# Splitting the softmax-denominator finish of an attention kernel into two steps, two strips apart

## The chip, the cores and the metric

One Trainium2 chip. The program runs on all 8 cores, each with one of the 8 batch elements and no exchange between them. The time is device time in microseconds (us) of the slowest core.

## The reference

One pre-norm transformer layer on x of 8 x 2048 x 1024 in f32. The first half is causal attention with 16 heads of 64 numbers and learned relative-position tables for keys and for values. The second half is a mixture of 8 experts of which each token takes the best one.

```
rel = jnp.tril(idx[:, None] - idx[None, :])
rk = embk[rel]
rv = embv[rel]
att = jnp.einsum('bhtd,bhsd->bhts', q, k) * scale + jnp.einsum('bhtd,tsd->bhts', q, rk)
att = jnp.where(causal[None, None], att, -jnp.inf)
att = jax.nn.softmax(att, axis=-1)
y = jnp.einsum('bhts,bhsd->bhtd', att, v) + jnp.einsum('bhts,tsd->bhtd', att, rv)
...
x = x + _L0_attn_ref(_layernorm(x, axis=-1), ...)
x = x + _L0_ffn_ref(_layernorm(x, axis=-1), ...)
```

The tables have 1024 entries, so a distance over 1023 reads the last one.

## The kernel before

Every instruction is written out by hand with the semaphores that it waits for, through one helper (`EM`, line 61 of the profile is its call). Each engine runs its instructions in the order in which they are written, so the order of the code is the order of each queue.

**Stages.** Layer norm and transposing of x; then for each group of 4 heads the projections to q, k, v; the attention of each of the 16 heads; the output projection; a second layer norm; the router; the experts (from about 3130 us on).

**A head.** It has a first part, in which q times the key table is computed for 16 row blocks, and stored to HBM (`prev_sb` to `prevh`). From there it is read back shifted by one element for each row, so that the distance becomes the position (`rel_sb`, loads on ScalarE's queue). Then come 16 strips of 128 query rows each, i = 0 to 15. Strip i does for each of its i // 4 + 1 chunks of 512 keys: TensorE makes scores (`ps_s<-qkv_sb`), VectorE adds `rel_sb` to them, ScalarE takes the exponential into `att_sb`. SyncE stores the strip shifted to `bmath`. The traversal of a strip (`trav_closure`) is written two strips later: TensorE transposes `att_sb` to `ps_t`, VectorE copies that to `attT_sb`, TensorE multiplies it with `vaug_sb` into `ps_y`. `vaug_sb` has v and two columns of ones, which give the sum of the exponentials, the softmax's denominator, in rows 64 and 65.

**The finish.** After strips 3, 7, 11 and 15, SyncE issues eight transposing loads of the stored exponentials (`bt_sb<-bmath`). Four strips later, ahead of strips 7, 11, 15 and of strip 3 of the next head, the finish of these four strips runs (`fin_closure`, line 640, kept in `pending_fin` with the strip at which it is due, lines 485 and 691):

- TensorE: eight matmuls `ps_y<-bt_sb,e_sb`, each waiting for its own load.
- ScalarE: `fin_sb<-ps_y`, copies the denominator rows out.
- VectorE: the cast `finb_sb<-fin_sb`, and the reciprocal `fin_sb<-fin_sb` of one row of 512.
- TensorE: `ps_y<-finb_sb,ev_sb`, the correction for distances beyond the table. Its wait is for VectorE's last instruction, the reciprocal.
- TensorE: `ps_s<-fin_sb,ones_f`, which replicates the reciprocal row to 64 partitions, in f32, into one of the four banks `ps_s` that the scores use in turn (`pool_alloc`).
- ScalarE: `rep_sb<-ps_s`, the copy of it; VectorE: `yT<-ps_y,rep_sb`, the multiplication.

There are two accumulators `ps_y`, which the groups of four strips use in turn, and 64 finishes in all. The finish of strips 8 to 11, for example, is ahead of strip 15; the accumulator that it frees is next written at the end of strip 2 of the next head.

Of the kernel before, what the change touches and what calls it, by code (L numbers as in the profile page):

```python
# [67 lines left out]
def build(debug=False):  # L68
# [33 lines left out]
    EM = P.emit  # L102

    with ExitStack() as gctx:
# [17 lines left out]
        cst_sb = E(nc.sbuf_tensor("cst_sb", [128, 8], F32))  # L122

        s_const = SM("s_const")
        s_pe = SM("s_pe")
        s_act = SM("s_act")
        s_dve = SM("s_dve")
# [39 lines left out]
        EM("vector", "memset", cst_sb[:, 4:5], -32.0, incs=[(s_dve, 1)])  # L167
        EM("vector", "memset", negbig_bf[:], NEGBIG, incs=[(s_dve, 1)])
        CONST_D = s_const.n
# [42 lines left out]
        with ExitStack() as actx:  # L212
# [23 lines left out]
               incs=[(s_dve, 1)])  # L236
            MS_D2 = s_dve.n

            for p in range(2):
                for g16 in range(16):  # L240
# [4 lines left out]
                       waits=([(s_dve, MS_D)] if (p == 0 and g16 == 0) else []),  # L245
                       incs=[(s_pg, 16)])
            PG_D = s_pg.n

            for p in range(2):
                for i8 in range(8):  # L250
# [4 lines left out]
                       waits=([(s_dve, MS_D)] if (p == 0 and i8 == 0) else []),  # L255
                       incs=[(s_bz[p], 16)])
# [6 lines left out]
            def pool_alloc():  # L263
                k = pool_ctr[0] % 4
                pool_ctr[0] += 1
                return k
# [8 lines left out]
            pending_fin = []  # L275
# [4 lines left out]
            fin_pe_guard = [0]  # L280
            plast_dve = [0]
# [6 lines left out]
            for i in range(NT):  # L288
# [5 lines left out]
                   waits=[(s_dve, xt_free[sl])], incs=[(s_x[sl], 16)])  # L294
# [9 lines left out]
            if debug:  # L304
                EM("gpsimd", "dma_start", out=dbg["dbg_xnT"], in_=xnT[:],
                   waits=[(s_act, P1_ACT)], incs=[(s_dbg, 16)])
# [17 lines left out]
            for g in range(4):  # L324
                par = 0
                wbase = 0
                for jout in range(6):
                    j3, mh = jout // 2, jout % 2
                    for tc in range(4):
# [7 lines left out]
                           waits=[(s_wq[0], wq_ready[g]), (s_act, max(P1_ACT, bg[0])),  # L337
                                  (s_dve, bg[1])],
                           incs=[])
# [26 lines left out]
                for hl in range(4):  # L366
                    h = 4 * g + hl
# [109 lines left out]
                    for i in range(NT):  # L477
# [147 lines left out]
                        if i % 4 == 3:  # L625
# [14 lines left out]
                            def fin_closure(tc=tc, ypar=ypar, h=h, hpar=hpar,  # L640
                                            btvals=tuple(btvals)):
                                for rt in range(8):
# [11 lines left out]
                                   waits=[(s_pe, max(yrel_pe, fin_pe_guard[0]))],  # L654
# [4 lines left out]
                                   incs=[(s_dve, 1)])  # L659
                                EM("vector", "reciprocal", fin_sb[64:65, 512:1024],  # L660
                                   fin_sb[64:65, 0:512], incs=[(s_dve, 1)])
                                fdv = s_dve.n
# [3 lines left out]
                                   waits=[(s_dve, fdv), (s_const, CONST_D)],  # L666
                                   incs=[(s_pe, 1)])
                                rbk = pool_alloc()
# [4 lines left out]
                                   waits=[(s_act, rbg[0]), (s_dve, rbg[1])],  # L673
# [17 lines left out]
                            pending_fin.append((gstrip + 4, fin_closure))  # L691

# [407 lines left out]
```

How the kernel before makes its waits and increments, by code:

```python
        def fn(h, method=method, args=args, kw=kw, wl=wl, il=il):  # L58
            for sh, v in wl:
                h.wait_ge(sh, v)
            ins = getattr(h, method)(*args, **kw)
            for sh, k in il:
                ins.then_inc(sh, k)
# [949 lines left out]
            def _final(h, OUT0=OUT0, OUT1=OUT1, DBG_D=s_dbg.n):  # L1013
                h.wait_ge(s_out[0].h, OUT0)
                h.wait_ge(s_out[1].h, OUT1)
                if DBG_D:
                    h.wait_ge(s_dbg.h, DBG_D)
```

## Time and profile before

| what | us |
|---|---|
| median of three runs | 5174.56 |
| the three runs | 5296.69, 5125.42, 5174.56 |
| the profiled execution | 5125.42 |
| its span, slowest core (core 0) | 5123.6 |
| spans of the eight cores | 5070.2 to 5123.6 |
| TensorE busy with matmuls | 3523.7 (69%) |
| VectorE busy | 1323.9 (26%) |
| ScalarE busy | 1283.8 (25%) |

The span runs from a core's first to its last instruction. PE is TensorE, PEld its weight loads, DVE VectorE, ACT ScalarE, SP SyncE; a q behind a name is an engine's sequencer, which issues transfers. In rows of groups the number behind the count is busy time, then the mean of one in ns, then the idle time of the engine just before them and what ended it. In rows of a timeline come the start, the length, the engine, the operation and in brackets the idle time before. Matmuls are pipelined: one that lasts 0.60 us makes room for the next after 0.43 to 0.47 us here.

### The profile page before, as it was taken

What the parts mean: (1) busy time and instruction counts of PE and PEld (TensorE: products, weight loads), DVE (VectorE), ACT (ScalarE), POOL (GpSimd) and SP (SyncE); (2) the same over time, 40 slices, a digit from 0 to 9 for tenths busy, and PEclk for the clock granted to TensorE, in tenths of its full rate; (3) what the DMA queues carried; (4) which work ended last, traced back from release to release, by engine and by line L of the source; (5) the groups of instructions that cost most, each with busy time, mean ns of one, the idle gap of its engine ahead of it and who ended that gap; (6) DMA issues with size and microseconds to landing.
All of it is one profiled execution on the core that took longest, in us unless ns stands there. A gap on an engine that the chain in (4) does not pass through costs nothing.

```text
span 5123.6 us, 48552 instructions; the slowest of 8 cores (5070.2 to 5123.6 us)
## 1 busy us (share of the span) xinstructions
PE 3523.7 (69%) x16065; PEld 1590.9 (31%) x16065; DVE 1323.9 (26%) x2366; ACT 1283.8 (25%) x2210; POOL 213.5 (4%) x373
## 2 busy tenths in 40 slices
PE   0455557555575566565665611999999999999992
PEld 0222223222232222222222200444444444444440
DVE  0134343434433444424444211001101110110011
ACT  3423223222222232233223042221121122112210
POOL 1000000000001000000000001000000000000002
PEclk9855556555565555565555855999999999999995
DMA  5255433443435333433444323130303113030303
GB/s 127 63 107 124 102 112 81 127 109 105 112 94 127 105 112 108 114 83 110 120 107 122 130 67 63 20 66 1 66 1 66 33 34 66 1 66 1 66 1 127
DMA packets 455408, 415.87 MB, mean 81 GB/s; under 512 B 304464, under 2 KB 353632, under 8 KB 455160
## 3 DMA queue, kind: packets, MB, share of 16 engines
q1 hardware_dynamic: 372992, 258.06, 18.2%
q0 software_dynamic: 45312, 76.06, 9.0%
q10 hardware_dynamic: 36864, 78.66, 6.1%
q8 instruction: 138, 2.26, 0.2%
q14 instruction: 102, 0.84, 0.1%
HBM read 264.16 MB, written 157.29 MB: 82 GB/s over the span
## 4 chain that ended last, share of the span: by engine, by line
PE 52%; DMA 15%; DVE 10%; SPq 7%; ACT 7%; issue 7%; POOL 1%; ACTq 1%; DVEq 0%; POOLq 0%
PE ps_h L61 17%; PE ps_v L61 17%; PE ps_s L61 9%; SPq L61 7%; PE ps_y L61 6%; DMA prevh<-prev_sb 6%; DVE fin_sb L61 4%; DMA bt_sb<-bmath 3%; DMA bmath<-att_sb 2%; DVE ps_s L61 2%; PE ps_t L61 2%; DMA xt_sb<-x 1%; ACT prev_sb L61 1%; DVE attT_sb L61 1%; ACT xn_sb L61 1%
## 5 line engine op out<-in xcount | busy, mean ns | idle before, releaser
L61 PE MATMUL ps_v<-w_sb,h_sb 128*128 128x512 bf16 x4096 | 889.2, 379 | 34.0 <-ACT h_sb L61 34.0
L61 PE MATMUL ps_h<-xn2T,w_sb 128*128 128x512 bf16 x4096 | 891.3, 380 | 30.1 <-DMA w_sb<-w 30.0
L61 ACT ACTIVATE h_sb<-ps_h,b1c_sb 128x512 bf16<-128x512 f32 x512 | 351.7, 687 | 1459.6 <-PE ps_h L61 1459.6
L61 DVE SCALAR_TENSOR_TENSOR acc_sb<-ps_v,g_sb,acc_sb 128x512 bf16<-128x512 f32 x256 | 192.4, 751 | 1649.0 <-PE ps_v L61 1649.0
L61 PEld LDWEIGHTS ps_v<-w_sb,h_sb 128*128 128x128 bf16 x4096 | 398.4, 98 | 524.8 <-issue 48.9
L61 PEld LDWEIGHTS ps_h<-xn2T,w_sb 128*128 128x128 bf16 x4096 | 400.9, 98 | 515.4 <-issue 33.9
L61 PE MATMUL ps_y<-attT_sb,vaug_sb 128*66 128x128 bf16 x2176 | 328.7, 305 | 289.9 <-DVE attT_sb L61 283.2
L61 ACT ACTIVATE att_sb<-ps_s,cst_sb 128x512 bf16<-128x512 f32 x640 | 395.3, 685 | 461.5 <-DVE ps_s L61 340.7
L61 DVE TENSOR_TENSOR ps_s<-ps_s,rel_sb 128x512 f32<-128x512 f32 (+3 forms) x624 | 386.4, 670 | 335.7 <-PE ps_s L61 327.0
L61 PE MATMUL ps_s<-embkRT_sb,qkv_sb 64*128 64x512 bf16 x448 | 202.7, 572 | 211.8 <-DVE plast_sb L61 108.4
L61 PEld LDWEIGHTS ps_y<-attT_sb,vaug_sb 128*66 128x66 bf16 x2176 | 228.7, 164 | 381.1 <-issue 378.2
L61 PE MATMUL ps_t<-eye_sb,att_sb 128*128 128x128 bf16 x2176 | 314.5, 308 | 14.3 <-ACT att_sb L61 14.3
L61 PE MATMUL ps_s<-qkv_sb 64*128 64x512 bf16 x640 | 312.9, 622 | 0.0
L61 DVE COPY attT_sb<-ps_t 128x512 bf16<-128x512 bf16 (+3 forms) x640 | 227.4, 379 | 303.0 <-PE ps_t L61 296.3
L61 PE MATMUL ps_y<-bt_sb,e_sb 128*66 128x512 bf16 x512 | 235.6, 597 | 90.4 <-DMA bt_sb<-bmath 89.7
L61 PEld LDWEIGHTS ps_t<-eye_sb,att_sb 128*128 128x128 bf16 x2176 | 218.4, 141 | 218.5 <-issue 218.5
L61 ACT CAST prev_sb<-ps_s 128x512 bf16<-128x512 f32 x256 | 146.5, 583 | 417.8 <-DMA prevh<-prev_sb 303.1
L61 PE MATMUL ps_y<-finb_sb,ev_sb 2*64 2x512 bf16 x64 | 38.2, 597 | 294.4 <-DVE fin_sb L61 294.4
L61 DVE RECIPROCAL fin_sb<-fin_sb 1x512 f32<-1x512 f32 x64 | 213.5, 3336 | 0.0
L61 DVE CAST prev_sb<-ps_s 128x512 bf16<-128x512 f32 (+1 forms) x192 | 119.8, 625 | 314.4 <-DMA prevh<-prev_sb 312.8
L61 PE MATMUL ps_s<-xnT,wqkv_sb 128*128 128x512 bf16 x768 | 172.0, 388 | 1.2 <-ACT xnT L61 1.2
L61 POOL DMA_DIRECT2D w_sb<-w x192 | 101.5, 592 | 1521.7 <-PE ps_h L61 1345.2
(83 smaller groups left out, 1401.2 us busy)
## 6 DMA issues: line engine op xcount, KB each, us to landing
w_sb<-w POOLq DMA_DIRECT2D x64, 512.0 KB, 13.5
w_sb<-w POOLq DMA_DIRECT2D x128, 256.0 KB, 10.8
prevh<-prev_sb SPq DMA_DIRECT2D x80, 384.0 KB, 2.3
rel_sb<-prevh ACTq DMA_DIRECT2D x80, 384.0 KB, 3.6
bmath<-att_sb SPq DMA_DIRECT2D x80, 384.0 KB, 3.0
xt_sb<-x SPq DMA_DIRECT2D x32, 512.0 KB, 4.0
rel_sb<-prevh ACTq DMA_DIRECT2D x64, 256.0 KB, 3.6
xt_sb<-x_spill SPq DMA_DIRECT2D x32, 512.0 KB, 3.8
```

Source lines behind the costliest of these rows:

```text
L61: ins = getattr(h, method)(*args, **kw)
```

## The change

The finish is written as two closures. The first, due at four strips as before, ends with the correction matmul, and that matmul waits for the cast alone. The second, due at six strips, has the replication, its copy and the multiplication; the replication now waits for its reciprocal by name. So the second halves stand ahead of strips 9, 13, and of strips 1 and 5 of the next head. ScalarE's copy into `fin_sb` waits also for the reciprocal of the finish before. One more constant is set at the start, which nothing reads.

```diff
+        EM("vector", "memset", cst_sb[:, 5:6], 0.0, incs=[(s_dve, 1)])
...
+            fin_war_dve = [0]
+            fin_rec = [0]
...
                                 EM("scalar", "copy", fin_sb[64:66, 0:512],
                                    ps_y[ypar][64:66, :],
-                                   waits=[(s_pe, max(yrel_pe, fin_pe_guard[0]))],
+                                   waits=[(s_pe, max(yrel_pe, fin_pe_guard[0])),
+                                          (s_dve, fin_war_dve[0])],
                                    incs=[(s_act, 1)])
...
+                                fdv_cast = s_dve.n
                                 EM("vector", "reciprocal", fin_sb[64:65, 512:1024],
                                    fin_sb[64:65, 0:512], incs=[(s_dve, 1)])
-                                fdv = s_dve.n
+                                fin_war_dve[0] = s_dve.n
+                                fin_rec[0] = s_dve.n
                                 EM("tensor", "matmul", ps_y[ypar][0:64, :],
                                    ev_sb[64:66, :], finb_sb[64:66, 0:512],
                                    start=False, stop=True, skip_group_check=True,
-                                   waits=[(s_dve, fdv), (s_const, CONST_D)],
+                                   waits=[(s_dve, fdv_cast), (s_const, CONST_D)],
                                    incs=[(s_pe, 1)])
+
+                            def fin_closure_b(tc=tc, ypar=ypar, h=h,
+                                              fin_rec=fin_rec):
                                 rbk = pool_alloc()
                                 rbg = pool_state[rbk]
                                 EM("tensor", "matmul", pool_banks[rbk][0:64, :],
                                    ones_f[64:65, :], fin_sb[64:65, 512:1024],
                                    start=True, stop=True,
-                                   waits=[(s_act, rbg[0]), (s_dve, rbg[1])],
+                                   waits=[(s_act, rbg[0]), (s_dve, fin_rec[0]),
+                                          (s_dve, rbg[1])],
                                    incs=[(s_pe, 1)])
...
                             pending_fin.append((gstrip + 4, fin_closure))
+                            pending_fin.append((gstrip + 6, fin_closure_b))
```

What the queues hold at the two kinds of place. TensorE in the first head, before: strip 13 with the traversal of strip 11 (first five rows), then further on the finish ahead of strip 15 and the strip's four scores.

```order
L61 MATMUL ps_s<-qkv_sb 128x512 x4
L61 MATMUL ps_t<-eye_sb,att_sb 128x128 x8
L61 MATMUL ps_y<-attT_sb,vaug_sb 66x128 x4
L61 MATMUL ps_t<-eye_sb,att_sb 128x128 x4
L61 MATMUL ps_y<-attT_sb,vaug_sb 66x128 x8
...
L61 MATMUL ps_y<-bt_sb,e_sb 66x512 x8
L61 MATMUL ps_y<-finb_sb,ev_sb 64x512
L61 MATMUL ps_s<-fin_sb,ones_f 64x512
L61 MATMUL ps_s<-qkv_sb 128x512 x4
```

The same two places after.

```order
L61 MATMUL ps_s<-fin_sb,ones_f 64x512
L61 MATMUL ps_s<-qkv_sb 128x512 x4
L61 MATMUL ps_t<-eye_sb,att_sb 128x128 x8
L61 MATMUL ps_y<-attT_sb,vaug_sb 66x128 x4
L61 MATMUL ps_t<-eye_sb,att_sb 128x128 x4
L61 MATMUL ps_y<-attT_sb,vaug_sb 66x128 x8
...
L61 MATMUL ps_y<-bt_sb,e_sb 66x512 x8
L61 MATMUL ps_y<-finb_sb,ev_sb 64x512
L61 MATMUL ps_s<-qkv_sb 128x512 x4
```

The replication `ps_s<-fin_sb,ones_f` has moved from behind the correction to the front of a strip: the one ahead of strip 13 belongs to the finish that began ahead of strip 11.

VectorE in the second head, from its first additions over the finish ahead of strip 3 to strip 5, before.

```order
L61 TENSOR_TENSOR ps_s<-ps_s,rel_sb 128x512 x3
L61 COPY attT_sb<-ps_t 128x128
L61 CAST finb_sb<-fin_sb 2x512
L61 RECIPROCAL fin_sb<-fin_sb 1x512
L61 TENSOR_TENSOR yT<-ps_y,rep_sb 64x512
L61 TENSOR_TENSOR ps_s<-ps_s,rel_sb 128x512
L61 COPY attT_sb<-ps_t 128x256
L61 TENSOR_TENSOR ps_s<-ps_s,rel_sb 128x512 x2
L61 COPY attT_sb<-ps_t 128x384
L61 TENSOR_TENSOR ps_s<-ps_s,rel_sb 128x512 x2
```

The same stretch after.

```order
L61 TENSOR_TENSOR ps_s<-ps_s,rel_sb 128x512
L61 TENSOR_TENSOR yT<-ps_y,rep_sb 64x512
L61 TENSOR_TENSOR ps_s<-ps_s,rel_sb 128x512 x2
L61 COPY attT_sb<-ps_t 128x128
L61 CAST finb_sb<-fin_sb 2x512
L61 RECIPROCAL fin_sb<-fin_sb 1x512
L61 TENSOR_TENSOR ps_s<-ps_s,rel_sb 128x512
L61 COPY attT_sb<-ps_t 128x256
L61 TENSOR_TENSOR ps_s<-ps_s,rel_sb 128x512 x2
L61 COPY attT_sb<-ps_t 128x384
L61 TENSOR_TENSOR yT<-ps_y,rep_sb 64x512
L61 TENSOR_TENSOR ps_s<-ps_s,rel_sb 128x512 x2
```

The reciprocal stays where it was, ahead of the next strip's addition. The multiplications `yT<-ps_y,rep_sb` stand now between the additions of strips 0 and 1 (for the finish ahead of strip 15 of the head before) and ahead of those of strip 5.

## Rows read from the trace of the kernel before

**Rows 1.** The page's chain that ended last, shares by engine and line.
```profile
PE 52%; DMA 15%; DVE 10%; SPq 7%; ACT 7%; issue 7%; POOL 1%; ACTq 1%; DVEq 0%; POOLq 0%
PE ps_h L61 17%; PE ps_v L61 17%; PE ps_s L61 9%; SPq L61 7%; PE ps_y L61 6%; DMA prevh<-prev_sb 6%; DVE fin_sb L61 4%; DMA bt_sb<-bmath 3%; DMA bmath<-att_sb 2%; DVE ps_s L61 2%; PE ps_t L61 2%; DMA xt_sb<-x 1%; ACT prev_sb L61 1%; DVE attT_sb L61 1%; ACT xn_sb L61 1%
```

**Rows 2.** Groups by shape, whole span: busy us, mean ns, idle before.
```profile
L61 PE MATMUL ps_y<-bt_sb,e_sb 128*66 128x512 bf16 x512 | 235.6, 597 | 90.4 <-DMA bt_sb<-bmath 89.7
...
L61 DVE RECIPROCAL fin_sb<-fin_sb 1x512 f32<-1x512 f32 x64 | 213.5, 3336 | 0.0
...
L61 PE MATMUL ps_y<-finb_sb,ev_sb 2*64 2x512 bf16 x64 | 38.2, 597 | 294.4 <-DVE fin_sb L61 294.4
```

**Rows 3.** Chain at a head's end, 1180 to 1345 us: start, length, what.
```profile
1188.99 2.37 DMA bmath<-att_sb
1191.44 2.01 SPq L61
...
1202.93 1.61 DMA prevh<-prev_sb
```

**Rows 4.** Timeline of the finish ahead of strip 15, 1336 to 1346 us.
```profile
1337.05 0.42 DVE L61 CAST finb_sb<-fin_sb 2x512 bf16<-2x512 f32 x1 [4.71 <-ACT fin_sb L61]
1337.39 3.34 DVE L61 RECIPROCAL fin_sb<-fin_sb 1x512 f32<-1x512 f32 x1
...
1340.88 0.60 PE L61 MATMUL ps_y<-finb_sb,ev_sb 2*64 2x512 bf16 x1 [4.59 <-DVE fin_sb L61]
...
1341.27 1.91 PE L61 MATMUL ps_s<-fin_sb,ones_f 1*64 1x512 f32 x2
...
1343.12 1.88 PE L61 MATMUL ps_s<-qkv_sb 64*128 64x512 bf16 x4
1343.27 0.58 ACT L61 COPY rep_sb<-ps_s 64x512 f32<-64x512 f32 x1 [6.33 <-PE ps_s L61]
...
1343.95 0.68 DVE L61 TENSOR_TENSOR yT<-ps_y,rep_sb 64x512 bf16<-64x512 f32 x1 [3.23 <-ACT rep_sb L61]
...
1344.56 0.74 DVE L61 TENSOR_SCALAR ps_s<-ps_s,plast_sb 128x512 f32<-128x512 f32 x1
```

**Rows 5.** Timeline of strip 13, 1320 to 1326 us.
```profile
1320.59 1.88 PE L61 MATMUL ps_s<-qkv_sb 64*128 64x512 bf16 x4
...
1321.30 0.43 DVE L61 TENSOR_TENSOR ps_s<-ps_s,rel_sb 128x256 f32<-128x256 f32 x1 [1.29 <-PE ps_s L61]
...
1323.82 0.75 DVE L61 COPY attT_sb<-ps_t 128x512 bf16<-128x512 bf16 x2
...
1324.39 0.61 PE L61 MATMUL ps_y<-attT_sb,vaug_sb 128*66 128x128 bf16 x4 [0.95 <-DVE attT_sb L61]
```

**Rows 6.** Timeline of a head's strips 0 to 2, 1237 to 1242 us.
```profile
1237.64 1.46 PE L61 MATMUL ps_s<-qkv_sb 64*128 64x512 bf16 x3
...
1238.36 1.90 DVE L61 TENSOR_TENSOR ps_s<-ps_s,rel_sb 128x512 f32<-128x512 f32 x3 [8.27 <-PE ps_s L61]
...
1240.36 0.23 DVE L61 COPY attT_sb<-ps_t 128x128 bf16<-128x128 bf16 x1
```

**Rows 7.** PE's waits in 2434:2443 (before strip 7), 2303:2317 and 1291.5:1301.5 (strip 11): total, times, longest.
```profile
PE ps_y L61 <- DMA bt_sb<-bmath: 2.0, 3, 1.3
...
PE ps_y L61 <- DMA bt_sb<-bmath: 0.3, 2, 0.2
...
PE ps_y L61 <- DMA bt_sb<-bmath: 4.7, 2, 2.4
```

**Rows 8.** The tile bt_sb: issue time in ns and landing in us, min/median/max.
```profile
L61 SPq DMA_TRANSPOSE bt_sb<-bmath x512: 1127/1261/3492, 278.2 to 2841.7; - x171
...
DMA to landing us min/median/max: 2.4/3.6/9.4
```

**Rows 9.** Windows: PE, PEld, DVE, ACT, POOL busy, granted clock, DMA share, GB/s.
```profile
1280.00:1360.00 80.00, 53.52 (x260) 27.20 (x260) 36.52 (x68) 21.10 (x36) 0.00 (x0) 0.54 0.53 109
...
1440.00:1520.00 80.00, 58.81 (x277) 29.31 (x278) 35.51 (x64) 24.03 (x40) 0.00 (x0) 0.60 0.44 112
```

## The prediction

> **What bounds the kernel now.** Read first the chain of work that ended last [rows 1]: TensorE (PE) holds 52%, but a third of that is the expert layers behind 3120 us, which the change does not touch. What matters are two items: "DVE fin_sb" with 4%, and "SPq" with 7%. The groups by shape come next [rows 2]. The reciprocal is one partition of 512 numbers, 3.34 us each, 64 of them, 213.5 us; 4% of 5124 us is 205, so nearly every one of them lies on the chain. The row of the matmul that reads finb_sb shows the same from PE's side: it stood idle 294.4 us before these 64, 4.6 us each.
>
> The timeline of one finish, the one ahead of strip 15, shows the order of things [rows 4]. The reciprocal runs from 1337.39 to 1340.73. PE then does the correction matmul (1340.88) and the replication matmul in f32 (1341.27, 1.91 us), and only then the scores of the strip (1343.12). ScalarE (ACT) copies the replicated row out (1343.27), VectorE (DVE) multiplies (1343.95), and DVE's first addition of the strip starts at 1344.56. So all three engines work on one thing after another here.
>
> Last, how a strip's exponentials reach the next event [rows 3]: at the end of a head they are followed by the store of att_sb, eight transposing loads that SyncE issues one by one from 1191.44, and the stores of prev_sb queued behind these at 1202.93. Each four strips inside a head have such a DMA chain too, and PE waits for its last piece: 89.7 us in 83 waits [rows 2].
>
> **The finish, first half.** After the change the correction matmul waits for the cast, which is over when the reciprocal starts, and PE goes on to the scores at once. For PE alone that brings the scores from 1343.12 to about the cast's end at 1337.47, plus 0.15 until PE has the signal and 0.39 for the correction: 1338.01, 5.1 us earlier [rows 4]. But the reciprocal keeps its place in DVE's queue, ahead of the additions, and PE's matmuls over attT_sb wait for a DVE copy that stands behind these additions. So the strip moves by what DVE gains: its first addition can start when the reciprocal ends, at 1340.73, and not at 1344.56. That is 3.83 us: the correction matmul, the replication, its copy and the multiplication. The reciprocal itself is not hidden. I take 3.83, the shift of the engine that ends last. The upper bound is PE's 5.1 us. Zero is excluded, since the reciprocals lie on the chain: the chain's 4% can be 3.5%, 179 of the 213.5 us, or 84% of them, and 84% of 3.83 is 3.2, the lower bound. It applies to 63 finishes (the 64th has no strip behind it; there only the correction matmul, 0.4 us, goes): 63 x 3.83 + 0.4 = 241.7 us. The exponentials of strips 3, 7, 11 and 15 come right behind a finish, so the DMA chains that they start move with them.
>
> **The second half, two strips later.** PE gets the replication ahead of the strip's scores, and DVE gets the multiplication ahead of its additions, behind ACT's copy. In rows 4 it takes 1344.56 - 1341.27 = 3.29 us from the replication's start to the first addition. Without it, at strip 13, it takes 1321.30 - 1320.59 = 0.71 us from scores to first addition [rows 5]. The price is 2.58 us where the DVE queue ends last, and it does there: the copy to attT_sb follows the additions (1323.82) and PE waits for it until 1324.39. It stands at strips 5, 9, 13 and 1 of the next head.
> - Strip 13: nothing covers it, since the finish ahead of strip 15 found its loads landed (there PE ran into them without a wait, its correction matmul follows at 1340.88). 16 x 2.58 = 41.3 us.
> - Strip 5: ahead of strip 7 PE waits for bt_sb anyway, at least 2.0 us [rows 7] and 58 us in the 16 heads. What is over the wait adds up to 1 us.
> - Strip 9: ahead of strip 11 these waits are 0.3 to 4.7 us [rows 7], 29 us in 16. Finish by finish, what 2.58 has over them adds up to 15.5 us.
> - Strip 1: three scores, three additions from 1238.36, a copy at 1240.36 [rows 6]. With the replication behind the first score (from 1238.07) the second addition starts at 1238.07 + 3.29 = 1241.36, the third 0.6 later, the copy at 1242.6: 2.2 us late. 15 x 2.2 = 33 us.
> Sum 91 us, with bounds 0 (all of it covered) and 63 x 2.58 = 163.
>
> **The rest.** The extra memset of a constant is one of six of its kind at the start and waits for nobody. The added wait of ACT's copy for an earlier reciprocal, and the replication's wait for its own, are met two strips before; behind them would stand the exponentials and the scores. A bank of ps_s is taken at another strip, one in four, free before the fourth score asks. These edits cost nothing, or at most their issue, below 0.1 us for each finish, 6 us.
>
> **Sum.** 241.7 - 91 = 150 us less. The profiled execution took 5125.4 us (span 5123.6): 4975. The median of the three runs, 5174.6, lies 49 above it: 5025 for a median of like runs. I set down 4995, between them. With the bounds of both halves the fastest is 5125 - 63 x 5.1 = 4804, the slowest 5125 - (63 x 3.2 - 163 - 6) = 5092, or 5141 on the scale of the median.
>
> **A rule of the clock.** The granted clock in this stage is 0.54 in one stretch of 80 us and 0.60 in another [rows 9], so mostly 1.2 GHz with patches of 2.4. The finishes' idle time on PE becomes shorter. The Trainium skill ("TensorE: Matmul & The Clock Gate", the part on HAM oscillation) says that an engine that keeps waiting between bursts falls back to half clock and pays the way up again, and one kept busy stays at full clock. By that the change could gain more than my sum. The trace agrees in that the stage with the gaps is the slow one, but PE's wait for the attT_sb copy remains in each strip.
>
> **Rivals.**
> 1. The second half costs its full price everywhere, as the DMA chain shrinks with the strips and covers nothing: 163 - 9 (strip 1 is cheaper) = 154, leaving 88 us: 5037, within 2%. For it: the waits at strip 11 are small. Against: a chain started by a strip has a length of its own. 15%.
> 2. The reciprocal is hidden whole (DVE's additions are not what ends last): 63 x 5.1 - 91 = 230, 4895. Against it stands the copy behind the additions [rows 5]. 5%.
> 3. The clock: if the stage went from 0.54 to 0.60, matmuls would take 10% less. PE's items ps_s, ps_y and ps_t on the chain are 17%, 871 us [rows 1]: 87 more gained, 4888. It is what the rule above would do here. 8%.
> 4. Slower: strips that come earlier push their bias loads into the eight transposing loads. Landing goes from 3.6 to the 9.4 us seen at worst, and one issue of the eight takes 3.49 in place of 1.26 [rows 8]: 8.0 us at 32 joins (strips 7 and 11), 2.2 at the 16 ends of a head, 291 us; less 150 it is 5266, 2.8% slower. The gain is gone from half of that lengthening on, and 2% slower is reached at 253 of 291. It would show as more idle time of PE before ps_y<-bt_sb than now. 4%.
> The forecast itself has 68%.
>
> **Range.** 4915 to 5110: the lower end goes halfway to rivals 2 and 3, the upper holds rival 1 on the median's scale (5086) and a little run to run spread. About 2% is what a measurement of this kernel can tell from no change. Faster by over 2% (103 us): most of the forecast (63 of 68) and rivals 2 and 3, 76%. Within 2%: rival 1 and the rest of the forecast, 20%. Slower: 4%.
>
> **What would show it.** Right: the wait of the finb_sb matmul falls from 4.6 to about 1.3 us (copy and cast alone), and the reciprocals stay on the chain with 4%; the first addition follows the reciprocal at once; the idle time before ps_y<-bt_sb falls from 90 to some 27 us, as the second halves at strips 5 and 9 fill it (37 and 26 of it); PE's idle time before ps_y<-attT_sb grows by 5.1 - 3.83 at each first half and by 2.58 - 1.85 (PE's own delay by the replication) at each second, 2.0 x 63 or some 126 us. Wrong: fin_sb gone from the chain (rival 2), the bt_sb idle time up (rival 4), the clock of the stage above 0.58 (rival 3), or a span less than 100 us shorter with the bt_sb idle time near zero (rival 1).

## The result, and the profile after

| | before | after |
|---|---|---|
| median of all runs, us | 5125.4 (13 runs) | 5004.0 (12 runs) |
| fastest run | 5106.5 | 4980.9 |
| profiled execution | 5125.4 | 5044.6 |
| first to last finish, mean of 8 cores | 2528.4 | 2398.9 |
| the same, fastest and slowest core | 2513.9, 2552.5 | 2387.3, 2411.7 |

The ratio of after to before is 0.978, 95% interval 0.973 to 0.983: the changed kernel is faster, but whether by more than 2% is not decided. In some executions four cores, or all eight, show a lower granted clock and take some per cent longer; the ratios leave these out, and so does the measure below, which for the kernel with the old wait is read on cores 4 to 7 alone and for the changed kernel's repetition not at all.

The fourth row is the measure used below, called the stage. It runs from the first to the last correction matmul `ps_y<-finb_sb,ev_sb` of a core and takes in nearly all that the change touches. The cores of one kernel differ in it by 22 to 45 us, so that a mean of eight is good to some 4 us (an estimate: the standard deviation of the cores over the root of eight). Its two ends for core 0 stand in the row of that matmul under the tile finb_sb; before it is this one:

```profile
L61 PE MATMUL ps_y<-finb_sb,ev_sb x64: 372/601/603, 297.1 to 2849.5; 2*64 2x512 bf16 x64
```

and after, on core 0:

```profile
L61 PE MATMUL ps_y<-finb_sb,ev_sb x64: 371/372/602, 280.7 to 2667.9; 2*64 2x512 bf16 x64
```

So 129.5 us went on the mean of the cores, where the sum had 150. The difference of the fastest runs is 125.6. In the profiled execution the slowest core is core 5, 101 us behind core 0. Its stage is 24 us longer than core 0's, and its expert layers, from the first to the last `h_sb<-ps_h`, are 59 us longer, at a lower granted clock. So most of the 64 us that the profiled execution has over the fastest run lies in layers that the change does not touch. The windows over the expert layers, core 5 and then core 0, clock in the third column from the end:

```profile
3120.00:5042.00 1922.00, 1785.84 (x7889) 784.60 (x7887) 206.93 (x280) 334.57 (x487) 126.20 (x184) 0.93 0.20 40
```
```profile
3050.00:4941.00 1891.00, 1754.46 (x8057) 785.20 (x8055) 211.47 (x286) 340.75 (x496) 126.20 (x184) 0.97 0.20 40
```

The chain that ended last, from the page of the profile after (core 5), answers to [rows 1]:

```profile
PE 56%; DMA 13%; issue 8%; DVE 7%; ACT 6%; SPq 6%; POOL 1%; ACTq 1%; DVEq 0%; POOLq 0%
PE ps_v L61 18%; PE ps_h L61 18%; PE ps_s L61 10%; PE ps_y L61 7%; SPq L61 6%; DMA prevh<-prev_sb 6%; DVE ps_s L61 3%; PE ps_t L61 3%; DMA bt_sb<-bmath 3%; DMA bmath<-att_sb 2%; DVE attT_sb L61 2%; DMA xt_sb<-x 2%; ACT xn_sb L61 1%; ACT prev_sb L61 1%; DMA xt_sb<-x_spill 1%
```

"DVE fin_sb" with its 4% is gone from it. That looks as if the reciprocal had been hidden. It has not, and the timeline of the finish ahead of strip 15 (core 0, the head of [rows 4]) says why:

```profile
1253.84 0.42 DVE L61 CAST finb_sb<-fin_sb 2x512 bf16<-2x512 f32 x1 [4.68 <-ACT fin_sb L61]
1254.19 3.34 DVE L61 RECIPROCAL fin_sb<-fin_sb 1x512 f32<-1x512 f32 x1
...
1254.41 0.37 PE L61 MATMUL ps_y<-finb_sb,ev_sb 2*64 2x512 bf16 x1 [1.33 <-DVE finb_sb L61]
...
1254.71 1.03 PE L61 MATMUL ps_s<-qkv_sb 64*128 64x512 bf16 x4
...
1255.68 0.62 PE L61 MATMUL ps_t<-eye_sb,att_sb 128*128 128x128 bf16 x8
1257.56 0.76 DVE L61 TENSOR_SCALAR ps_s<-ps_s,plast_sb 128x512 f32<-128x512 f32 x1
...
1260.71 0.61 PE L61 MATMUL ps_y<-attT_sb,vaug_sb 128*66 128x128 bf16 x4 [4.41 <-DVE attT_sb L61]
```

PE's wait in front of the correction fell from 4.59 to 1.33 us, and the scores follow at once. But PE is through with scores and transposes at 1256.30 and then waits 4.41 us for the copy to attT_sb, which stands behind the additions, which stand behind the reciprocal: the first addition starts at 1257.56, the reciprocal ends at 1257.53. The wait has changed its place and its name. The chain of the same stretch shows how it loses the reciprocal:

```profile
1254.78 0.97 PE ps_s L61 x4
1255.75 0.34 PE ps_t L61 x4
...
1256.14 1.42 issue
1257.56 0.77 DVE ps_s L61
```

An addition is put down to the engine whose semaphore it waited for, PE, and the time in which VectorE was busy with the instruction before it becomes "PE ps_s", "PE ps_t" and "issue". The groups by shape, core 0, answer to [rows 2]:

```profile
L61 PE MATMUL ps_y<-attT_sb,vaug_sb 128*66 128x128 bf16 x2176 | 328.1, 304 | 454.6 <-DVE attT_sb L61 448.2
...
L61 PE MATMUL ps_y<-bt_sb,e_sb 128*66 128x512 bf16 x512 | 214.1, 572 | 41.7 <-DMA bt_sb<-bmath 41.0
L61 DVE RECIPROCAL fin_sb<-fin_sb 1x512 f32<-1x512 f32 x64 | 213.5, 3336 | 0.0
...
L61 PE MATMUL ps_y<-finb_sb,ev_sb 2*64 2x512 bf16 x64 | 28.9, 451 | 85.6 <-DVE finb_sb L61 85.6
```

Before the correction 209 us of idle time went (294.4 to 85.6), before ps_y<-bt_sb 49 (89.7 to 41.0). Before ps_y<-attT_sb PE's idle time rose to 448.2, from 283.2 before:

```profile
L61 PE MATMUL ps_y<-attT_sb,vaug_sb 128*66 128x128 bf16 x2176 | 328.7, 305 | 289.9 <-DVE attT_sb L61 283.2
```

The second half, ahead of strip 13 in the same head (core 0), answers to [rows 5]:

```profile
1234.80 1.97 PE L61 MATMUL ps_s<-fin_sb,ones_f 1*64 1x512 f32 x2
...
1236.69 1.88 PE L61 MATMUL ps_s<-qkv_sb 64*128 64x512 bf16 x4
1236.85 0.58 ACT L61 COPY rep_sb<-ps_s 64x512 f32<-64x512 f32 x1 [3.72 <-PE ps_s L61]
...
1237.53 0.68 DVE L61 TENSOR_TENSOR yT<-ps_y,rep_sb 64x512 bf16<-64x512 f32 x1 [3.31 <-ACT rep_sb L61]
...
1238.14 0.41 DVE L61 TENSOR_TENSOR ps_s<-ps_s,rel_sb 128x256 f32<-128x256 f32 x1
```

From the replication's start to the first addition it takes 3.34 us, 0.71 without one [rows 5]: 2.6 us, as priced.

Where the time went, by the finish that ends each cycle, mean in us over the cores and heads. The cycle is the distance to the finish before it, taken at the start of the last of the eight matmuls `ps_y<-bt_sb`.

| finish ahead of strip | before | after | change | forecast |
|---|---|---|---|---|
| 7 | 26.00 | 23.23 | -2.77 | -3.76 |
| 11 | 28.32 | 25.98 | -2.34 | -2.86 |
| 15 | 33.46 | 32.16 | -1.30 | -1.25 |
| 3 of the next head | 71.89 | 70.02 | -1.87 | -1.63 |

The forecast column is 3.83 less the second half's price at the strip in that cycle (0.07, 0.97, 2.58, 2.2). Over 16 heads the four differences add up to 132 us measured and 152 forecast. The two cycles that end in a wait for the transposing loads fall short; the other two do not.

Read transfer by transfer, the last of the eight transposing loads landed 3.36 us behind its issue ahead of strip 7 before and 4.34 after, and ahead of strip 11 4.06 and 4.65. That is as much as the 1.0 us missing at strip 7; whether it is the cause, the experiments below test. A bias load is a strip's load of rel_sb. The one that strip 6 issues (for strip 9) came 5.1 us behind the first transposing load before, and 7.6 after; strip 10's 7.3 and 10.0 (heads 2 to 16). The last transposing load is issued 9.2 us behind the first.

### The profile page after: what moved, and what is told of

Its sections match the earlier page's. It is cut to its first block, busy times and chain, and to the rows that moved or that the text cites. A ratio compares the mean times of both kernels' runs of the same rounds, so it can differ in the third digit from the quotient of the medians.

```text
span 5042.7 us, 48445 instructions; the slowest of 8 cores (4941.8 to 5042.7 us)
## 1 busy us (share of the span) xinstructions
PE 3552.9 (70%) x16065; PEld 1593.6 (32%) x16065; DVE 1329.3 (26%) x2367; ACT 1284.5 (25%) x2210; POOL 213.5 (4%) x373
## 4 chain that ended last, share of the span: by engine, by line
PE 56%; DMA 13%; issue 8%; DVE 7%; ACT 6%; SPq 6%; POOL 1%; ACTq 1%; DVEq 0%; POOLq 0%
PE ps_v L61 18%; PE ps_h L61 18%; PE ps_s L61 10%; PE ps_y L61 7%; SPq L61 6%; DMA prevh<-prev_sb 6%; DVE ps_s L61 3%; PE ps_t L61 3%; DMA bt_sb<-bmath 3%; DMA bmath<-att_sb 2%; DVE attT_sb L61 2%; DMA xt_sb<-x 2%; ACT xn_sb L61 1%; ACT prev_sb L61 1%; DMA xt_sb<-x_spill 1%
## 5 line engine op out<-in xcount | busy, mean ns | idle before, releaser
L61 PE MATMUL ps_v<-w_sb,h_sb 128*128 128x512 bf16 x4096 | 924.9, 390 | 33.8 <-ACT h_sb L61 33.8
L61 PE MATMUL ps_h<-xn2T,w_sb 128*128 128x512 bf16 x4096 | 924.6, 390 | 28.2 <-DMA w_sb<-w 28.2
L61 PE MATMUL ps_s<-qkv_sb 64*128 64x512 bf16 x640 | 295.1, 584 | 0.0
L61 PE MATMUL ps_y<-bt_sb,e_sb 128*66 128x512 bf16 x512 | 222.4, 589 | 41.4 <-DMA bt_sb<-bmath 41.1
L61 DVE RECIPROCAL fin_sb<-fin_sb 1x512 f32<-1x512 f32 x64 | 213.5, 3336 | 0.0
L61 PEld LDWEIGHTS ps_s<-embkRT_sb,qkv_sb 64*128 64x128 bf16 x448 | 43.3, 105 | 330.8 <-issue 324.2
```

Source lines behind the costliest of these rows:

```text
L61: ins = getattr(h, method)(*args, **kw)
```

## The experiments

The stage is given as in the table above (first to last finish, mean of 8 cores); the changed kernel has 2398.9. Ratios are to the kernel before, with their 95% intervals.

### Each edit alone

First the changed kernel with the second half back behind the first.

```diff
-                            pending_fin.append((gstrip + 6, fin_closure_b))
+                            pending_fin.append((gstrip + 4, fin_closure_b))
```

> The changed kernel with its second half back at four strips, directly behind the first: of the change only the wait for the cast in place of the reciprocal is left. Theory A (the strip waits for VectorE's queue, the replication waits for the reciprocal anyway): only the correction matmul leaves the chain, 0.4 us x 63 = 25 us less than the kernel before, about 5086. Rival C (PE's 4.6 us wait was the bound, and ending it is the gain): 3.3 us x 64 = 209 us less, about 4900.

Measured: ratio 0.998 (0.993 to 1.003), stage 2523.7, that is 4.7 us less than before, no more than the two means can be off. PE's wait ahead of the correction is 1.33 us here too, but of the 209 us of idle time that the weaker wait could be thought to end nothing comes back: the replication stands right behind and waits for the reciprocal. Theory A had 25 us. The first exponential of the strip does come 0.4 us earlier behind the reciprocal's end (4.3 where it was 4.7); but only the cycle ahead of strip 15 is shorter by 0.4, the others are not. This kernel also has all the small edits that the prediction priced under "the rest" (the constant, the added waits), and they cost nothing that shows.

Now the changed kernel with the old wait.

```diff
-                                   waits=[(s_dve, fdv_cast), (s_const, CONST_D)],
+                                   waits=[(s_dve, fin_rec[0]), (s_const, CONST_D)],
```

> The second half at six strips as in the changed kernel, but the correction matmul waits for the reciprocal as before. Theory A: the first addition comes 1.0 us after the reciprocal's end (correction 0.15 + 0.4, first score 0.5) where the changed kernel has it at once, 63 x 1.0 = 63 us slower than the changed kernel, about 5045; so the move is worth about half of the gain and the weaker wait the other half, but only once the second half is away. Rival C: the weaker wait carries all, and this kernel is as slow as the one before, 5111.

Measured: ratio 0.990 (0.985 to 0.996), stage on cores 4 to 7 2492.8 (2501.7 on all eight). The same four cores had 2523.1 before and 2406.7 in the changed kernel: 30 less and 86 more. Theory A's 63 was too little: the first exponential comes 1.35 us later than in the changed kernel, not 1.0, and 63 of these are 85. Rival C falls too. The two edits alone gain 4.7 and 30 us, together 129.5. The move pays its price at the later strip in any case, and its gain at the finish is full only where the correction doesn't stand behind the reciprocal.

### Is the reciprocal still on the path

A second one of the same row into a scratch tile, ahead of the real one.

```diff
+                                EM("vector", "reciprocal", dum_sb[64:65, 0:512],
+                                   fin_sb[64:65, 0:512],
+                                   waits=[(s_dve, dum_war[0])], incs=[(s_dve, 1)])
+                                dum_war[0] = s_dve.n
                                 EM("vector", "reciprocal", fin_sb[64:65, 512:1024],
                                    fin_sb[64:65, 0:512], incs=[(s_dve, 1)])
```

> The changed kernel with a second reciprocal of the same row into a scratch tile, ahead of the real one. Theory A: each second one is on the chain too, 3.3 us x 63 = 208 us more than the changed kernel: 5190, and as many us more from first to last finish. Rival C (hidden behind PE's work): 4985.

Measured: ratio 1.016 (1.008 to 1.024), stage 2611.5: 212.6 us more. The second reciprocals are busy for

```profile
L61 DVE RECIPROCAL dum_sb<-fin_sb 1x512 f32<-1x512 f32 x64 | 213.5, 3336 | 0.0
```

so every one of them counts in full. And the other way round, the reciprocal as exp(-ln(x)) on ScalarE:

```diff
-                                EM("vector", "reciprocal", fin_sb[64:65, 512:1024],
-                                   fin_sb[64:65, 0:512], incs=[(s_dve, 1)])
...
+                                EM("scalar", "activation", fin_sb[64:65, 512:1024],
+                                   fin_sb[64:65, 0:512], AF.Ln,
+                                   waits=[(s_act, fav)], incs=[(s_act, 1)])
+                                EM("scalar", "activation", fin_sb[64:65, 512:1024],
+                                   fin_sb[64:65, 512:1024], AF.Exp, scale=-1.0,
+                                   waits=[(s_act, s_act.n)], incs=[(s_act, 1)])
...
```

> The changed kernel with the reciprocal taken by ScalarE as exp(-ln(x)), two instructions of about 0.6 us, in place of VectorE's 3.34 us. Theory A (the reciprocal is still in front of the strip's additions and on the chain): the first addition then waits for the first score, 1.25 us behind the cast instead of 3.27, 2.0 us x 63 = 126 us less than the changed kernel: 4858. Rival C (the change has hidden the reciprocal): 4985.

Measured: ratio 0.954 (0.944 to 0.963), stage 2276.2: 122.7 us less than the changed kernel, against 126 expected. The timeline of the finish ahead of strip 15, core 0:

```profile
1208.47 1.34 ACT L61 ACTIVATE fin_sb<-fin_sb 1x512 f32<-1x512 f32 x2
1208.48 0.42 DVE L61 CAST finb_sb<-fin_sb 2x512 bf16<-2x512 f32 x1 [3.48 <-ACT fin_sb L61]
...
1209.04 0.37 PE L61 MATMUL ps_y<-finb_sb,ev_sb 2*64 2x512 bf16 x1 [1.33 <-DVE finb_sb L61]
...
1209.35 1.03 PE L61 MATMUL ps_s<-qkv_sb 64*128 64x512 bf16 x4
1209.84 0.76 DVE L61 TENSOR_SCALAR ps_s<-ps_s,plast_sb 128x512 f32<-128x512 f32 x1 [0.95 <-PE ps_s L61]
```

The first addition starts 0.94 us behind the cast's end, where it was 3.3. Now it waits for the first score. The Trainium skill ("ScalarE: Activation LUTs", on table sets) says that one set holds exp and ln, so that going from one to the other needs no table load; the trace agrees, it has one load in the whole span, as before.

### What the second half costs

The replication and its copy are left out, and the multiplication becomes a plain copy.

```diff
-                                EM("tensor", "matmul", pool_banks[rbk][0:64, :],
-                                   ones_f[64:65, :], fin_sb[64:65, 512:1024],
...
-                                EM("scalar", "copy",
-                                   rep_sb[0:64, (tc % 2) * 512:(tc % 2 + 1) * 512],
...
-                                EM("vector", "tensor_tensor",
+                                EM("vector", "tensor_copy",
...
```

> The changed kernel without the replication: no reciprocal row is spread and ps_y is only copied to yT (0.6 us on VectorE) at six strips, so the division by the denominator is left out. It prices the second half. Theory A: from the cycles between finishes of the changed kernel it costs 2.5 us at strip 13, 1.9 at strip 1, 1.4 at strip 9 and 1.0 at strip 5, with the landing that it lengthens; 5.6 us a head come back (the 0.6 of the copy stays at strips 13 and 1), 90 us: 4895, from first to last finish 2309. By the prediction's prices (2.58, 2.2, 0.97, 0.07) 70 us would come back: 4915. Rival D: nothing comes back, 4985.

Measured: ratio 0.957 (0.948 to 0.965), stage 2321.6: 77.3 us come back, between the prediction's 70 and the cycles' 90. The cycles say where:

| finish ahead of strip | changed kernel | without replication | comes back | prediction's price |
|---|---|---|---|---|
| 7 | 23.23 | 22.94 | 0.29 | 0.07 |
| 11 | 25.98 | 25.03 | 0.95 | 0.97 |
| 15 | 32.16 | 29.77 | 2.39 | 2.58 |
| 3 of the next head | 70.02 | 68.79 | 1.23 | 2.2, of which 0.6 stays |

So the prediction's four prices stand, the one of strip 5 (in the cycle ahead of strip 7) too: it is 0.29 us a head, not the 1.0 that the expectation read from the cycles. By these numbers what is short is the first half's gain. With no replication at all, the first two cycles are 3.06 and 3.29 us shorter than in the kernel before, where the first half alone was priced at 3.83. Together that is 1.3 us a head, 21 us in all, as much as the whole sum lacks. Both are the cycles whose end waits for the transposing loads. PE's wait for these loads is 88.7 us on the mean of the cores here, 74.8 before and 40.4 in the changed kernel. In the cycle ahead of strip 7 the way from the last exponential of strip 3 to the last landing takes 15.5 us before (heads 2 to 16), 16.2 here, 16.6 in the changed kernel, and 16.0 in the kernel with the weaker wait alone, whose strips hardly moved. So these transfers took longer in all of these kernels than in the one before; why, and how much of it is a difference between executions, stays open.

The last landing ahead of strip 7 is 3.62, the one ahead of strip 11 4.03, nearly as before the change. So the lengthened landing goes with the second half in front of a strip, and not with the finish being earlier.

### Which transfer is in the way

The second half one strip later:

```diff
-                            pending_fin.append((gstrip + 6, fin_closure_b))
+                            pending_fin.append((gstrip + 7, fin_closure_b))
```

> The second half stands seven strips after its group instead of six: ahead of strips 10, 14, and of 2 and 6 of the next head. Theory A: the second half at strip 5 pushes the bias load that strip 5 issues (rel_sb for strip 8) from 2.0 to 4.6 us behind the first transposing load, onto the last ones, whose landing went from 3.4 to 4.4 us; placed at strip 6 it leaves that load alone. Then the last landing ahead of strip 7 returns to about 3.4 us, the one ahead of strip 11 from 4.65 to about 4.1, and the kernel is about 25 us faster than the changed one: 4957. Rival B: the landing lengthened for another reason (transfers of all cores denser in time): landing stays 4.4 and 4.65, time 4982, as the changed kernel.

Measured: ratio 0.972 (0.965 to 0.979), stage 2399.5, no gain where 25 us were expected. Theory A of this run falls as it was put: strip 5's load went back to 1.8 us behind the first transposing load, and yet the last one landed after 4.03 us (strip 7) and 4.74 (strip 11). But strip 6's load stayed late, at 7.4, as did strip 10's at 9.8. Beside it ran the changed kernel once more.

> The changed kernel once more, on the same chip as the others, as their reference: 4980 to 4990 us; from first to last finish about 2399 us on the mean of the cores.

Measured: ratio 0.974 (0.968 to 0.979), which can't be told from the 0.972 one strip later. The runs behind this ratio took 4998.1 to 5015.8 us, 8 to 26 more than the upper end that was expected.

The kernels whose second half does not delay strips 6 and 10 (the weaker wait alone, the one without the replication, and one at the end of the next section that has both halves at four strips) have strip 6's load at 4.7 to 4.8 us and the landing at 3.4 to 3.6. The move alone, which does delay them, has 7.6 and 4.27. So the next experiment moves only the bias loads, ahead of their strip's exponentials:

```diff
+                        if i + 3 < NT:
+                            issue_rel(i + 3)
                         chunk_act = [0] * nch
...
-                        if i + 3 < NT:
-                            issue_rel(i + 3)
```

> The changed kernel with each strip's bias load (rel_sb, for the strip three later) issued ahead of the strip's exponentials on ScalarE's queue instead of behind them, 1 to 3 us earlier; everything else stays. Theory E: the last transposing load lands late (4.3 us ahead of strip 7, 4.65 ahead of strip 11, where it was 3.4 and 4.1) because the second halves push the load issued at strips 6 and 10 onto it, 7.6 and 10.0 us behind the first transposing load instead of 5.1 and 7.3. Then the loads go out at about 6.2 and 7.8, the landings fall to about 4.0 and 4.3, and the stage is some 16 x 0.5 = 8 us shorter: 2391. Rival: the landing does not follow that load, and stays at 4.3 and 4.65, 2399.

Measured: ratio 0.968 (0.961 to 0.974), stage 2395.0. The loads went out 4.3 and 5.5 us behind the first transposing load, and the landings fell to 3.54 and 4.08, nearly as before the change. PE's wait for these loads on core 0 is

```profile
PE ps_y L61 <- DMA bt_sb<-bmath: 30.2, 38, 3.3
```

where the changed kernel had 41.0. That late bias loads lengthen the transposing loads' last landing is thereby shown. What it is worth is less: the cycle ahead of strip 7 gained 0.5 us, the one ahead of strip 11 0.1, and the cycle over the head's end lost 0.4, for a reason that stays open. So 4 us are left of it, no more than the means can be off. A part is given back on the way: the first transposing load now goes out later behind the last exponential of strips 3 and 7, by 0.3 and 0.4 us.

### A better place, and the best kernels

The replication is written inside the traversal of the same strip, between the transposes and the matmuls over attT_sb; the multiplication behind the traversal.

```diff
...
                             for q4 in range(1, ngr):
                                 pv = emit_trans(q4)
+                                if q4 == 1 and pending_b:
+                                    mul = pending_b.pop(0)()
                                 emit_avs(q4 - 1)
                                 emit_copy(q4, pv)
                             emit_avs(ngr - 1)
+                            if mul:
+                                mul()
...
```

> Both halves belong to the same strip again, but the replication is written inside the strip's traversal, between its transposes and its matmuls over attT_sb, where PE waits for VectorE anyway (the additions stand behind the reciprocal), ScalarE's copy behind the strip's exponentials, and the multiplication behind the traversal's copies. Theory A (a strip is bound by VectorE's queue; the second half costs 2.5 us where it stands in front of a strip, and next to nothing where its engines are waiting): all of the first half's 63 x 3.8 = 239 us is kept less about 18 us (at strip 3 with one chunk the replication ends 0.9 us after PE could go on, at strip 7 0.2), so 221 us less than the kernel before, 4890; no strip's bias load is shifted, so the last landing ahead of strip 7 returns to 3.4 us and the one ahead of strip 11 to 4.1. Rival D: what the changed kernel lacks against its sum is lost in the transfers, whose chain sets the pace: no faster than the changed kernel, 4985, landings of 4.4 and 4.7.

Measured: ratio 0.956 (0.951 to 0.961), median 4912.5, stage 2319.3: 79.6 us less than the changed kernel, where 91 had been expected, with the same instructions. The finish ahead of strip 15, core 0:

```profile
1240.79 3.34 DVE L61 RECIPROCAL fin_sb<-fin_sb 1x512 f32<-1x512 f32 x1
...
1246.12 1.93 PE L61 MATMUL ps_s<-fin_sb,ones_f 1*64 1x512 f32 x2 [3.21 <-DVE ps_s L61]
1246.74 0.76 DVE L61 COPY attT_sb<-ps_t 128x512 bf16<-128x512 bf16 x2
...
1247.98 0.64 PE L61 MATMUL ps_y<-attT_sb,vaug_sb 128*66 128x128 bf16 x4
```

The replication stands in PE's own wait, but not all of it: at a strip with four chunks it takes the bank of ps_s that the strip's first score had. That bank is free after this score's exponential, which ends at 1245.76 by the trace (the row names an addition, but the one of this bank was over at 1244.92). So the replication starts only at 1246.12, and PE goes on 0.7 us after the copy for which it would otherwise have waited (1246.74 + 0.42 + 0.15 = 1247.31). The expectation had missed the bank; PE's wait for it adds up to 48.7 us on the mean of the cores. The landings are 4.03 and 4.56, not the 3.4 and 4.1 expected, so this gain did not need them. Ahead of strip 7 the bias load is late here too, at 6.2 us. Ahead of strip 11 it is at 7.3, as before the change, and the landing is 0.5 us longer than before all the same: something besides this load counts there, and no run isolates it.

With ScalarE's exp(-ln(x)) in addition:

> The threaded second half together with ScalarE's exp(-ln(x)) in place of the reciprocal. Theory A: the two gains are of the same kind and add up in part. With ScalarE's form alone the stage from first to last finish is 2276 us; there the second half still costs some 6 us a head at strips 13, 1, 9 and 5. Threaded, the replication's 1.85 us stand against the 0.95 us that PE waits at that place, about 0.9 us at each of four finishes: 2.4 us a head less, 40 us: stage 2236, time about 4820. Rival D (what is left is set by the transfers' chain): no gain on ScalarE's form alone, 4865.

Measured: ratio 0.927 (0.921 to 0.934), median 4789.1, stage 2200.4, 75.8 us less than with ScalarE's form alone, nearly twice the 40 expected; where the other half comes from was not traced. PE's wait for the bank is 9 us here in place of 48.7. And with the second half directly behind the first:

> ScalarE's exp(-ln(x)), with the second half back directly behind the first, as in the kernel before: what the split is worth once the long reciprocal is gone. Theory A: replication ends at 0.9 + 1.9 us behind the cast, copy 3.5, multiplication 4.2, then the first addition, where it was 7.1 before: 63 x 2.9 = 183 us less than the kernel before, stage 2346, time 4930, some 65 us slower than ScalarE's form with the split. Rival: with the reciprocal short, the split no longer pays, 4865.

Measured: ratio 0.961 (0.952 to 0.970), stage 2359.4: 83.2 us slower than with the split. The split pays also where the reciprocal is short. Last, with the reciprocal row in bf16:

```diff
-                                EM("scalar", "activation", fin_sb[64:65, 512:1024],
+                                EM("scalar", "activation", recb_sb[64:65, :],
                                    fin_sb[64:65, 512:1024], AF.Exp, scale=-1.0,
...
-                                   ones_f[64:65, :], fin_sb[64:65, 512:1024],
+                                   onesb_sb[64:65, :], recb_sb[64:65, :],
```

> As the threaded kernel with ScalarE's exp(-ln(x)), and the reciprocal row is written in bf16 and spread by a bf16 matmul of 512 columns, 0.43 us of PE's time in place of 1.85. Theory A: the replication then fits into PE's wait of 0.95 us and costs nothing: 0.9 us x 63 = 57 us less than the f32 form, stage about 2180, time about 4765. Rival D: the transfers' chain takes over (PE's wait for bt_sb grows by as much): 4820.

Measured: ratio 0.926 (0.919 to 0.934), median 4796.5, stage 2184.5. Of the 57 us expected against the f32 form 15.9 came in the stage, and the times can't be told apart. On the mean of the cores PE's wait for bt_sb grew from 74.9 to 88.3 us and its wait for attT_sb from 188.4 to 220.6: about a third of the missing 41 us went where rival D had it, the rest into waits for VectorE's copies.

## Why the prediction was right, and where its terms were off

Measured were 5004.0 us for 4995 forecast, inside the range, and 129.5 us of gain in the stage for a sum of 150. The step on which most hung, that the strip moves by what VectorE gains and not by PE's 5.1 us, held. That the time came within 9 us is in part luck. The 4995 stands 20 us above the sum's own 4975 because the median of three runs of the kernel before lay 49 above the profiled execution; with more runs that median is 5125.4, the profiled execution's time, so these 20 us had no ground, and they made up for the 20 that the sum had too much. The forecast of a gain over 2% (76%) is neither confirmed nor refuted by an interval of 0.973 to 0.983.

One reading was wrong without effect: the expert layers are not a third of PE's 52% on the chain but two thirds, ps_h and ps_v with 34% [rows 1].

- **First half, 3.83 us for each of 63.** Right for the strip, too much for the time. The strip's first exponential came 4.67 us behind the reciprocal's end before and 0.88 after, 3.79 less, on the mean of cores and finishes. That the reciprocal is not hidden is shown by both experiments on it, +212.6 us for a second one and -122.7 us for taking it off VectorE. But in the cycles whose end waits for the transposing loads the shift did not arrive whole: without the replication the cycles ahead of strips 7, 11 and 15 are 3.06, 3.29 and 3.69 us shorter than before. The prediction let the DMA chains "move with" the exponentials at no cost, and in the changed kernel the one ahead of strip 7 took 1.0 us longer.
- **Second half at strip 13, 2.58 us.** Right: 2.6 in the timeline, and the cycle ahead of strip 15 is 1.30 us shorter where 3.83 - 2.58 = 1.25 was forecast.
- **At strip 1, 2.2 us.** Slightly too much: 3.79 - 1.87 = 1.9, and 1.8 by the kernel without the replication (1.23 come back, 0.6 of the copy stays).
- **At strip 9, 15.5 us in all.** Right by the kernel without the replication, 0.95 us a head for 0.97, with some luck. The step took PE's waits ahead of strip 11 from the profiled slowest core, where they add up to 28.8 us; on the mean of the cores it is 19.9 over 16 heads, 1.24 each, and what 2.58 has over them, finish by finish, is 1.37. That 0.95 was paid and not 1.37 would fit transfers that took longer; no run tests it. The cycle is 0.5 us a head short of its forecast, 8 us in all, and that is the first half's share.
- **At strip 5, 1 us in all.** Nearly right: 0.29 us a head by the kernel without the replication, 5 us in all. "PE waits for bt_sb anyway" was true, and the wait covered the 2.58 us. The cycle ahead of strip 7 is 1.0 us short, 16 us in all. In the changed kernel this is the last landing, 1.0 us longer, as the delayed strips issue their bias loads onto the last transposing load. But taking the second half away or issuing the loads early brings the landing back and only 0.3 or 0.5 us of the cycle. So the bias loads are one part, and the other part of what lengthens these transfers is open. This is rival 4's place (bias loads against transposing loads) at a fraction of its price, and its reason, the earlier finish, does not hold for the landing: that one goes with the second half.
- **The signs to look for.** PE's wait before the correction 1.33 us: right. The reciprocals in the chain with 4%: wrong, though they are on the path; the view puts a wait behind a busy engine down to the semaphore's giver, and the sign that the prediction gave for rival 2 (fin_sb gone from the chain) came although rival 2 is refuted. Idle time before bt_sb: 27 forecast, 41.0 measured on core 0, mostly through the later landing; with the early loads it is 30.2. Idle time before attT_sb: 126 more forecast, 165 measured on core 0; part of this is PE's faster clock at that place, the rest was not traced.
- **Rival 3, the clock.** The granted clock of the stage rose a little. Core 0, 300 to 2600 us, before and after:

```profile
300.00:2600.00 2300.00, 1394.43 (x6172) 629.58 (x6171) 901.18 (x1666) 667.05 (x1136) 29.56 (x56) 0.56 0.42 109
```
```profile
300.00:2600.00 2300.00, 1433.42 (x6557) 654.87 (x6557) 970.68 (x1782) 711.89 (x1210) 29.55 (x56) 0.58 0.44 116
```

  The correction matmul's median of 372 ns in place of 601, and four scores in 1.03 us where they took 1.88 [rows 4], say where: right behind the finish, where PE's idle stretch went from 4.6 to 1.3 us. Over these scores the granted clock is 1.00 (2.4 GHz), where it was 0.50 (1.2 GHz). The Trainium skill ("TensorE: Matmul & The Clock Gate", on HAM oscillation) says that an engine that waits between its bursts starts the next one at half clock; this trace agrees. It brought next to nothing, since at that place PE is early anyway and waits 4.41 us for VectorE.
- **Rivals 1 and 2.** Rival 1 (nothing is covered, 63 us more) did not come: the second half costs 0.29 us ahead of strip 7 and 0.95 ahead of strip 11, not 2.58. Rival 2 is refuted by the second reciprocal.

## What to carry to other kernels

A wait that is weakened helps only as far as nothing else holds the same work: before it is priced, look for the next instruction of the waiting engine that needs the busy one, and count everything in that one's queue. What is moved out of a hand-off between engines costs its round trip again where it is put in front of other work (2.4 of 2.6 us here at strip 13), unless a later wait covers it (0.3 at strip 5). So put it where its engines already wait, and look at which transfers the delayed work issues. Where a chain of transfers is started earlier and its end is waited for, do not count on the whole shift arriving (3.1 and 3.3 of 3.8 us here). A long instruction on a single partition (one row of 512 in 3.34 us) can hold up a whole engine's queue; try it on the engine with room.

## What the runs showed of the hardware

- A reciprocal of 512 f32 numbers takes VectorE 3336 ns on one partition, eight times the cast of two such rows on two partitions (418). Logarithm and exponential of the same row take ScalarE 1.34 us together.
- Transposing loads from HBM land later when a plain load of the same core meets them. Ahead of strip 7, with a load of 384 KB, the last of eight landed after 3.4 to 3.6 us when that load was issued 4.3 to 5.1 us behind the first, and after 3.8 to 4.6 when it was issued 5.3 to 7.7 us behind it. Moving the loads early in the same kernel brought 4.34 back to 3.54. Ahead of strip 11 the picture is less clear: 4.0 to 4.6 us with the load at 7.0 to 7.5.
- After an idle stretch of 1.3 us instead of 4.6 ahead of it, PE's burst at the finish ran at 2.4 GHz and no longer at 1.2 (granted clock 1.00 and 0.50 ahead of strip 15, median of the correction matmul 372 and 601 ns). The stage's mean granted clock is 0.58 still, so mostly 1.2 GHz.
